# Attention layer of a three-layer network in sixteen rounds, with projections as three fp32r products

## The reference

```python
ln_out = layernorm(hidden_states, ln1_s, ln1_b)            # [8, 256, 512]
q, k, v = jnp.split(ln_out @ w_qkv + b_qkv, 3, axis=-1)
ctx = merge_heads(attention(split_heads(q), split_heads(k), split_heads(v), ltor_mask))
x = hidden_states + ctx @ w_ao + b_ao
q = layernorm(x, ln2_s, ln2_b) @ w_q + b_q
k, v = jnp.split(encoder_states @ w_kv + b_kv, 2, axis=-1)
ctx = merge_heads(attention(split_heads(q), split_heads(k), split_heads(v), cross_mask))
x = x + ctx @ w_co + b_co
x = x + gelu(layernorm(x, ln3_s, ln3_b) @ w1 + b1) @ w2 + b2
```

## Time and profile before

| | |
|---|---|
| median of three runs | 2108.29 us (2104.38 to 2113.11) |
| the profiled execution, its own time | 2109.36 us |
| its span in the profile | 2107.6 us |
| granted TensorE clock, mean | 0.94 of 2.4 GHz |

### The profile page before, as it was taken

One profiled execution on the slowest core, in us unless ns is written; L12 is line 12 of the kernel. 1 busy time (PEld: TensorE's weight loads), 2 busy tenths in 40 slices (PEclk: granted clock), 3 DMA queues, 4 the chain that ended last, 5 costly groups with the idle time before them and its releaser, 6 DMA issues. The chain is left out here.

```text
span 2107.6 us, 32615 instructions
## 1 busy us (share of the span) xinstructions
PE 1866.5 (89%) x12032; PEld 1211.1 (57%) x12032; DVE 1185.9 (56%) x2735; ACT 1053.9 (50%) x2298; POOL 137.7 (7%) x95
## 2 busy tenths in 40 slices
PE   4779999999999965689999999999988759999999
PEld 2334344343443323467677766777756438999988
DVE  5567565675756511447767676776666436333332
ACT  2346665656656641447666666666656434111121
POOL 3011010100000000000000000000000000000000
PEclk8779999999999987799999999999999889999999
DMA  5222222222122005554464645445451333000000
GB/s 171 75 73 82 87 72 72 77 91 84 53 69 73 17 11 180 141 141 122 105 151 106 149 111 126 116 121 126 111 130 41 91 97 115 26 21 21 21 21 21
DMA packets 159374, 185.36 MB, mean 88 GB/s; under 512 B 25072, under 2 KB 115312, under 8 KB 159216
## 3 DMA queue, kind: packets, MB, share of 16 engines
q1 hardware_dynamic: 159216, 183.27, 32.0%
HBM read 119.78 MB, written 63.44 MB: 87 GB/s over the span
## 5 line engine op out<-in xcount | busy, mean ns | idle before, releaser
L732 DVE TENSOR_REDUCE a_mx<-a_mscore 128x2 f32<-128x1024 f32 x256 | 313.1, 1223 | 212.5 <-PE a_mscore L428 211.3
L584 ACT ACTIVATE a_pt<-a_escore 128x1024 f32<-128x1024 f32 x256 | 262.2, 1024 | 172.6 <-PE a_escore L416 172.2
L1391 ACT ACTIVATE b_pr<-b_t,b_nmax 128x256 f32<-128x256 f32 x512 | 253.9, 499 | 182.7 <-DVE b_nmax L1501 182.7
L1497 DVE TENSOR_TENSOR b_t<-b_score,b_mask 128x1024 f32<-128x1024 f32 x128 | 156.0, 1219 | 155.9 <-PE b_score L1279 155.7
L1501 DVE CUSTOM_DVE_ANT_0 b_t<-b_t,b_minus 128x256 f32<-128x256 f32 x512 | 197.1, 441 | 16.9
L1818 ACT ACTIVATE c_gT<-c_d,c_b 128x256 f32<-128x256 f32 x128 | 53.8, 471 | 265.3 <-PE c_d L1743 265.3
L1403 ACT ACTIVATE b_pt<-b_d 128x512 f32<-128x512 f32 x256 | 138.8, 592 | 76.4 <-PE b_d L1291 71.5
L416 PE MATMUL a_escore<-a_qst,a_kst 50*128 50x512 f32 x512 | 134.2, 519 | 37.7 <-ACT a_pt L584 37.5
L416 PEld LDWEIGHTS a_escore<-a_qst,a_kst 50*128 50x128 f32 x512 | 50.5, 192 | 195.2 <-ACT a_pt L584 98.2
L1291 PE MATMUL b_d<-b_ident,b_pr 128*128 128x128 f32 x1024 | 141.5, 279 | 19.9 <-DVE b_cxT L1521 8.0
L428 PE MATMUL a_mscore<-a_kst,a_qst 48*128 48x512 f32 x512 | 117.8, 454 | 35.8 <-DVE a_mx L732 27.5
(11 more groups left out here) (137 smaller groups left out, 3271.7 us busy)
## 6 DMA issues: line engine op xcount, KB each, us to landing
b_qst<-b_q SPq DMA_DIRECT2D x96, 256.0 KB, 5.1
b_kst<-b_k SPq DMA_DIRECT2D x96, 256.0 KB, 7.1
b_q<-b_parts SPq DMA_DIRECT2D x64, 256.0 KB, 2.8
b_k<-b_parts SPq DMA_DIRECT2D x64, 256.0 KB, 2.8
a_qst<-a_q_parts SPq DMA_DIRECT2D x192, 64.0 KB, 2.2
a_kst<-a_k_parts SPq DMA_DIRECT2D x192, 64.0 KB, 2.2
a_q_parts<-a_qparts SPq DMA_DIRECT2D x32, 256.0 KB, 2.3
a_k_parts<-a_kparts SPq DMA_DIRECT2D x32, 256.0 KB, 2.2
```

Source lines behind the costliest of these rows:

```text
L584: nc.scalar.activation(pt[:, at % RING, :, :], escore[:], ACT.Exp, scale=SCALE).then_inc(exp_done.sem, 1)
L732: nc.vector.tensor_reduce(mx[:, q, 2 * pair:2 * pair + 2], mscore[:], AX_X, ALU.max).then_inc(max_done.sem, 1)
L1391: last = nc.scalar.activation(pr[:, u % 2, j, :], t[:, u % 2, j, :], ACT.Exp, scale=-1.0, bias=nmax[:, u, j:j + 1], accum_out=esum[:, u, j ...
L1497: nc.vector.tensor_tensor(t[:, u % 2], score[:, u % 2].rearrange("p x (y n) -> p (x y) n", y=2), mask[a][:, q, :].unsqueeze(1).broadcast_t ...
```

## The change

Before, `i` steps over batches with sixteen positions. After, `v` steps over sixteen rounds of eight positions: rounds 0 to 7 are the self-attention of batches 0 to 7, rounds 8 to 15 their cross-attention. Every tile that had one instance for each attention has one for both.

- The result of self-attention is stored to `mid_out`. A cross round loads it again, once as `xt` for the layer norm and once as `xr` for the residual. Self rounds load the hidden input twice too.
- Four weight matrices lie in SBUF at a time, each as a high and a low part. `high_weight` (ScalarE) and `low_weight` (VectorE) make them. The second four come through one tile `stage` in rounds 5 to 8.
- Every projection is three products of parts: high by high, high by low, low by high.
- The parts of the normalised input, of the encoder states and of the context are made by pairs `turned_high` and `turned_low`, `encoded` and `encoded_low`, `context_high` and `context_low`. Those of q and k are made straight from PSUM, half a projection at a time, by `high` and `low`, which replace `biased` and `split`; `context_high` and `context_low` add the value bias too, in place of `value_bias`.
- The bank of a q, k or encoder fill is now released by the second of the pair, on VectorE.
- `weigh` and `divide` take two units at a time, every second position. The transposed probabilities have three slots for two. `val` has two slots by round.
- The factor 1/sqrt(32) goes into the mask, by one more instruction in `set_mask`.

The core of the diff, and the order of the new positions:

```diff
     SELF, CROSS = 0, 1
-    FIRST, LAST = -3, B
-    POSITIONS = range(2 * NU)
+    ROUNDS = 2 * B
+    FIRST, LAST = -2, ROUNDS
...
         FILL = {
-            0: [(("turn", 0, u), 2) for u in range(2)],
-            1: [(("q", 0, 0), 2)],
-            2: [(("o", 1, t_), -1) for t_ in range(TT)],
...
+            0: [("q", 1, 1)],
+            1: [("k", 1, 1)],
+            2: [("v", 0, 1)],
+            3: [("v", 1, 1), ("enc", 0, 2), ("enc", 1, 2)],
+            4: [("o", 0, -1)],
+            5: [("turn", 0, 2), ("turn", 1, 2), ("o", 1, -1)],
+            6: [("q", 0, 2)],
+            7: [("k", 0, 2)],
         }
...
+        read = {"pt": pt_done, "w": cx_done, "q": qk_low[0], "k": qk_low[1], "v": v_done, "o": x_done}
...
                     for k in range(KT):
-                        mm = nc.tensor.matmul(at[:, j * S:(j + 1) * S], w[:, k, m:m + P], src[:, k, :],
-                                              start=(k == 0), stop=(k == KT - 1))
+                        for c, (x, y) in enumerate(((0, 0), (0, 1), (1, 0))):
+                            mm = nc.tensor.matmul(at[:, j * S:(j + 1) * S], w[:, x, k, m:m + P], src[:, y, k, :],
+                                                  start=(k == 0 and c == 0), stop=(k == KT - 1 and c == 2))
...
+            def high(v, which, h):
...
+                qk_out[which][before[1]].need(act, before[0], 2)
+                qk_filled[which].need(act, v, h + 1)
+                for j in range(2):
+                    k = 2 * h + j
+                    last = nc.scalar.activation(parts[which][:, 0, j, :], bank("qk"[which], v, h)[:, j * S:(j + 1) * S], ACT.Identity,
+                                                bias=bias_of(kind(v), which, k))
+                last.then_inc(qk_high[which].sem, 1)
...
+            def body(v):
+                for p in range(NU):
+                    keep(*unit_at(v, p))
+                    exponentials(*unit_at(v, p + 2))
...
+                    if p == 0:
+                        high(v + 1, 0, 1)
+                    if p == 1:
+                        if v == B - 2:
+                            high_weight(4)
+                        high(v + 1, 1, 1)
+                    if p == 2:
+                        context_high(v - 1, 1)
+                        value(v + 1, 0)
+                    if p == 3:
+                        value(v + 1, 1)
+                        encoded(v + 2)
...
+                    if p == 5:
+                        turned(v + 2)
+                        turned_high(v + 2)
+                    if p == 6:
+                        context_high(v, 0)
+                        if v == B:
+                            high_weight(7)
+                        high(v + 2, 0, 0)
+                    if p == 7:
+                        high(v + 2, 1, 0)
...
+            def low(v, which, h):
...
+                qk_high[which].need(dve, v, h + 1)
+                for j in range(2):
+                    k = 2 * h + j
+                    last = nc.vector.scalar_tensor_tensor(parts[which][:, 1, j, :], bank("qk"[which], v, h)[:, j * S:(j + 1) * S],
+                                                          bias_of(kind(v), which, k), parts[which][:, 0, j, :].bitcast(F32),
+                                                          ALU.add, ALU.subtract)
+                last.then_inc(qk_low[which].sem, 1)
...
+            def turned_low(v):
...
+                ln_high.need(dve, v, 1)
+                nc.vector.tensor_tensor(lnp[:, 1], lnT[:], lnp[:, 0].bitcast(F32), ALU.subtract).then_inc(ln_low.sem, 1)
...
+                for p in range(NU):
+                    soften(*unit_at(v, p + 2))
+                    if p % 2 == 0:
+                        w, u = unit_at(v, p - 2)
+                        divide(w, u // 2)
+                    invert(*unit_at(v, p + 1))
...
+                    if p == 0:
+                        low(v + 1, 0, 1)
+                        normalise(v + 2)
+                    if p == 1:
+                        if v == B - 2:
+                            low_weight(4)
+                        low(v + 1, 1, 1)
+                        apply(v + 2)
+                    if p == 2:
+                        context_low(v - 1, 1)
+                    if p == 3:
+                        encoded_low(v + 2)
+                        set_mask(v + 1)
+                    if p == 4:
+                        residual_sum(v - 1, 0)
...
+                    if p == 5:
+                        turned_low(v + 2)
+                        residual_sum(v - 1, 1)
+                    if p == 6:
+                        context_low(v, 0)
...
+                        low(v + 2, 0, 0)
+                    if p == 7:
+                        low(v + 2, 1, 0)
```

More of the change, by code:

```diff
@@ L882, in unit, with unit_at, units_before, slot @@
         return half, tile, four
[L884 to L920, removed]
+    def unit_at(v, p):
+        return v + p // NU, p % NU
+    def units_before(n, v, u):
+        at = v * NU + u - n
+        return divmod(at, NU) if at >= 0 else None
+    def slot(v, u):
+        return (v * NU + u) % PTS
+    def mask_of(v):
+        return 0 if v < B else (v + 1) % 2
     with ExitStack() as ctx:
@@ L1165, in _ @@
+            for v in range(FIRST, LAST + 1):
+                body(v)
+            sp.wait_ge(x_out.sem, x_out.at(ROUNDS, 0))
         @block.gpsimd
@@ L1270, in scores @@
+            def scores(v, u):
+                if not there(v):
                     return
@@ new lines, in weigh @@
+                for x in range(2):
+                    u = 2 * pair + x
+                    inverse_done.need(pe, v, u + 1)
+                    for j in range(G):
+                        mm = nc.tensor.matmul(at[j * DH:(j + 1) * DH, (2 + x) * P:(3 + x) * P],
+                                              inverse[:, u, j:j + 1].broadcast_to([P, DH]), ident[:],
+                                              start=True, stop=True, tile_position=(0, j * DH))
+                mm.then_inc(pv_done.sem, 1)
@@ new lines, in value, with context_high @@
+                v_filled.need(act, v, t_ + 1)
+                nc.scalar.activation(val[v % 2][:, t_, :], bank("v", v, t_), ACT.Copy).then_inc(v_done.sem, 1)
+            def context_high(v, h):
+                if not there(v):
+                    return
+                o_filled.need(act, v - 1, TT)
+                cx_done.need(act, v, 2 * h + 2)
+                for k in range(2 * h, 2 * h + 2):
+                    last = nc.scalar.activation(cxp[:, 0, k, :], cx[:, k, :], ACT.Identity, bias=value_bias(kind(v), k))
+                last.then_inc(cx_high.sem, 1)
@@ new lines, in context_low, with residual_sum @@
+                for k in range(2 * h, 2 * h + 2):
+                    last = nc.vector.scalar_tensor_tensor(cxp[:, 1, k, :], cx[:, k, :], value_bias(kind(v), k),
+                                                          cxp[:, 0, k, :].bitcast(F32), ALU.add, ALU.subtract)
+                last.then_inc(cx_low.sem, 1)
+            def residual_sum(v, t_):
+                if not there(v):
+                    return
+                if t_ == 0:
+                    r_biased.need(dve, v, 1)
+                o_filled.need(dve, v, t_ + 1)
+                nc.vector.tensor_tensor(xr[:, t_, :], bank("o", v, t_), xr[:, t_, :], ALU.add).then_inc(x_done.sem, 1)
```

877 lines of the change are left out of this document (436 added, 441 removed).

## The result

The changed kernel takes 2175.73 us (median of 4 runs, 2165.98 to 2177.34); the kernel before took 2109.3 beside it. The ratio on record is 1.0294, 95% interval 1.0274 to 1.0313 (the two medians alone give 1.0315): 3% slower. The forecast was 2182. The profiled span is 2172.5 us.

What follows compares the result with a forecast made beforehand. TensorE bounds the kernel before; after, a chain through VectorE and ScalarE does. 2107.6 for the profiled span, plus 64 for the later layer end, plus 10 for the clock, gave 2182 us; own range 2140 to 2230, 8-in-10 range 2115 to 2250.

Steps and rivals of the forecast that it cites:

- What bounds the kernel: Layer's steady stretch: TensorE bound it before, at 96%; after the change its share falls to about 0.8.
- The handoff loop: One position on VectorE and ScalarE: `soften` and exponentials 4.84, `high` 0.85, handoffs 0.05, then `low`: 6.6 us.
- uncertain term: `low` on VectorE, two operations over 256 columns: 0.9 us a pair, bounds 0.7 and 1.5.
- One sign on record: VectorE would show idle time ended by ScalarE's parts, 3 to 4 us a position.
- The positions: Eight position lengths on VectorE summed to 55.3 us a self round and 59.0 a cross round.
- The edges: First scores at 860 us, within 6; with filling, rounds, second weights and emptying, layer end at 1773, 64 later.
- The clock: TensorE's granted clock falls; its fills in positions 2 to 4 are on the path: 8 to 15 us, 10 taken.
- Projections: Three fp32r products on TensorE: a call falls from 3.37 to 2.83 us, 69 us over eight batches.
- In order queues: ScalarE and VectorE queues are strict FIFO: nothing behind `low` passes it, 2182 us; without that rule 1990.
- TensorE as the bound (1990): Rival: exponentials run far enough ahead, a batch takes 91.3 us less 1 or 2, 1990 us; chance 0.09.
- partly hidden: Rival: mean handoff 6.0 us, or `o` in position 4 not waiting, saves 4 to 5 a round: 2110 us; chance 0.07.
- that rival (2238): Rival: waits take TensorE to its lower clock level a third of the time, 3 to 4 us a round: 2238; chance 0.09.

Runs made afterwards that it cites:

- all moves together: Changed kernel with `low` of q and k and `context_low` one position later on VectorE, and `turned` with `turned_high` ahead of the exponentials on ScalarE: 2076.88 us.
- With one product: Changed kernel with only the product of the high parts in all projections, the two other products left out: 2150.89 us.
- the experiment on the kernel before: Kernel before, each projection as three fp32r products of the same rounded operands, one rounded weight matrix for all, no splitting, one 1 MB load less: 2049.11 us.
- the first two experiments: Changed kernel with projections as one plain float32 matmul of the high parts, 2179.15 us; then with only the high by high product, 2150.89 us.
- the last kernel: Changed kernel with q/k `low` and `context_low` later, `turned` and `turned_high` before exponentials, `rsqrt` before `add_bias`, second k half's `low` back in position 1: 2008.22 us.

## Why the prediction was right, and where it was off

*What bounds the kernel.* Right: before, TensorE did; after, TensorE is busy for 80% of the stretch and a chain through the queues of ScalarE and VectorE sets the length of a round.

*The handoff loop.* Right in mechanism and size: 6.57 us against 6.6. Its uncertain term, `low`, is 0.87 us a pair against 0.9, and `high` 0.81 to 0.84 against 0.85. The edits that break handoffs, and change neither work nor engines, confirm it: the four `low` of q and k moved alone give 36 us, `turned` moved ahead alone 51 (45 of them behind the first scores), all moves together 99. One sign on record was off: VectorE was to wait 3 to 4 us a position for ScalarE's parts, and waits 2.0 to 2.8. The loop's own terms ask for 2.7 (exponentials to 4.84 and `high` 0.85, against 3.0 of VectorE's own work).

*The positions.* The step table stands beside its forecast: no self position is off by more than 0.2 us, and the self round is 55.1 against 55.3. The mean of rounds 6 to 13 is 60.1 against 59.0, as three of them (6, 7 and 9: 63.8, 61.6 and 61.5) hold the split of the second weights, which the forecast counted apart. The other five are 58.8 on the mean, and the three stand 10.6 above that in all, where 11 was forecast.

*The edges.* First scores at 862.75 (forecast 860, within 6). The layer ends at 1773.1; 1773 was forecast. What follows takes 399 us. That the end is hit to 0.1 us is luck: the start alone scatters by 8 us between profiles, and the four executions of the kernel by 11.

*The clock.* This term of 10 us was wrong, and the profiled span is 9.5 us below the forecast. The granted clock fell as expected (0.94 and 0.91 in the stretches), but the slower calls lie under the handoff loop: the call at 1097.37 took 1.55 us longer than the one at 1103.12 and the step over it, 1097.24 to 1105.55 on VectorE, was 8.31, as in the forecast without a clock term. From 973 to 1193 the first v call of each round, behind waits of 3.1 to 4.6 us, takes 4.2 to 5.3 us instead of 2.9, and its position is still 6.6. With one product the clock is 0.83 in self rounds and they are still 0.9 us shorter. I had argued that fills of positions 2 to 4 are on the path; with one product only p4 of those positions gets shorter, from 6.4 us to 5.4, and its o call, 2.81 to 2.84 us, ran at full clock (1.00 from 1125.06 to 1127.90). In the self rounds the calls that were slow were not on the path, and the one on the path was not slow.

*Projections.* The gain a call was put too high: 0.54 us from the network layer's pitch of 0.118, where these calls run at 0.122 and give 0.44. The v calls gain less: they took 3.03 to 3.14 us before, not 3.37, and take 2.88 to 2.90 at full clock. The gain a call doesn't enter the forecast, since the loop hides TensorE's work; in the experiment on the kernel before it shows as 0.46 a call on the mean. The rule of the Trainium skill quoted there (page "FP8 and Floating Point Precision", section "TensorE Precision Notes": four passes for true FP32, from which 2.53 us for three products is an estimate) is further from the 2.93 measured than the row was.

*In order queues.* The trace agrees with the Trainium skill, page "TensorE: Matmul & The Clock Gate", section "Architectural detail": nothing behind `low` passed it (`low` ends at 1112.12, `apply` and the next maxima follow). GpSimd's queue showed the same: `rsqrt` started at 1394.21, when the addition that had waited for a load was done, and moving it ahead gave 24 us.

*The rivals.* TensorE as the bound (1990) was excluded by the +3 and -25 us of the first two experiments. It is nearly what the last kernel reaches, 2008, once most waits of the handoffs are gone; it needed four kinds of operation moved. The loop was not partly hidden (6.57 us). The clock did fall to a mixture of its levels in single calls, but these were not on the path, so the time of that rival (2238) wasn't seen.

*What my experiments missed.* Two forecasts treated handoffs as if they added up, 2015 and 2080. They don't: a bank, a handoff and a result of another engine end in the same position, and the latest sets it. Releasing the bank of the second half of k gave 5 us or nothing (within scatter) while `context_low` was a handoff and 44 when it was not.

*Where the last kernel's gain lies.* In the self rounds of the last step the released bank and the faster call share the gain about equally, 1.5 us each; the slow call went together with the wait ahead of it, and whether it could go alone wasn't tried. The last kernel's batch, 93.2 us, is no shorter than the 92.6 of the old order with three products, and yet it is 41 us faster. The two traces show that this lies at the ends: its first scores come at 857.0 against 865.6, and from the first of its 128 `soften` the first sixteen take 84.8 us against 108.6 and the last sixteen 78.0 against 104.7, while the stretch between is 10 us longer.

*What stays open.* The cross rounds of the last step (3.0 us each) weren't taken apart in the same way. The old order was never timed with operands that are really split, so what that work would cost there isn't known, and the comparison with the last kernel is of the products and the order alone.

## What to carry to other kernels

When two engines hand work to each other in order, look for the operation that waits for something the other engine does later in the same position: it makes the position as long as both engines' work in sequence, and no busy share shows it (here no engine was above 84%). Put the second half of such a pair behind the next position's work, the first half ahead of what is long in its queue; but look first at who waits for the result or the bank, since an operation that the next fill needs must not move. Count a change in a shared position by what ends last there after it, and try moves together before one is called worthless.

## What the hardware showed that was not expected

At rounds of almost equal length (56.1, 55.1 and 54.2 us) the granted clock of the self stretch went with TensorE's busy time: 0.97 with plain float32 (189 of 220 us), 0.94 with three products (177), 0.83 with one (139). So work left out of a TensorE that waits was partly given back as slower matmuls. An estimate: the stretch holds 32 calls, 2.93 us each with three products and 1.02 with one at full clock, so some 61 us of busy time should have gone, and only 37 did.

A call of 24 products that started after a wait of 3.66 us took 4.48 us instead of 2.93, 0.187 us a product against 0.122, at a granted clock of 0.62 over the call, between the two levels. Not each such wait did it: the same call two rounds earlier, at 987.06, took 2.94 us after a wait of 3.65, with the clock at 1.00.

The float32 matmul over 256 columns takes 0.42 us in two records (3.37 us for eight), three fp32r products 0.366: a factor of 0.87, not three quarters.
